# A top-2 expert layer on one core: uneven halves in the second pass, and results sent to their tokens instead of fetched

## The chip, the cores and the metric

The kernel runs on one core of a Trainium2 chip. The metric is the device time of one execution, in microseconds (us). The kernel before has a median of 599.58 us over three runs (596.98 to 600.19).

## The reference, cut to what matters

Input x has 16 x 256 = 4096 tokens of 128 channels. The reference is a sandwich: half an expert layer, attention, and the same half expert layer again.

```python
x = x + 0.5 * ffn(layernorm(x))
x = x + attention(layernorm(x))          # 16 heads of 8, causal over 256 tokens
x = x + 0.5 * ffn(layernorm(x))

def ffn(xt):                             # 16 experts, the best 2 of each token
    logits = xt @ Wg.T + bg
    top_vals, top_idx = top_k(logits, 2)
    rw = softmax(top_vals)
    gate, up = interleaved halves of xt @ Wgu[e] + bgu[e]
    gate, up = minimum(gate, 7.0), clip(up, -7.0, 7.0)
    gated = (up + 1.0) * gate * sigmoid(1.702 * gate)
    return sum over the 2 experts of rw * (gated @ Wd[e] + bd[e])
```

## The kernel before, in words

**Tiles and groups.** The 4096 tokens are 32 tiles of 128. Four tiles are a group, so there are eight groups, 0 to 7 (`NQ`). Each expert layer works on two sides. In both layers a side is four groups: sides 0 and 1 in the first layer, 2 and 3 in the second.

**Routing.** For each group TensorE makes the logits, VectorE finds the two best experts, and from running counts computes for every (token, choice) a row in a DRAM buffer `rows_by_expert`. GpSimd then issues one indirect DMA per tile and choice (`scatter`, L600), eight for a group, which writes 128 normalised token rows to these places. Each expert has a region of its own per side. When a side's counts are known, VectorE makes a table that gives for each tile of expert work its first row and its expert; SyncE copies it into `tab` (L459).

**Expert passes.** A side is 48 expert tiles (32 tiles of choices and one more per expert for padding; 47 are run), two by two in 24 pairs, and four pairs make a turn. For each pair SyncE loads the rows (L467), TensorE transposes them (`turn_x`, L1793), ScalarE copies the transposes out of PSUM (`evac_x`, L883) and brings the weights (L876), TensorE multiplies (`gate_up`, L1805; `down`, L1817), VectorE gates (L1332 to L1335) and adds the bias (`evac_y`, L1349), and ScalarE stores the results to DRAM in tile order (`store`, L895). The five steps run staggered over consecutive slots of one pair each. Every engine's queue is a fixed order, written out by the program; semaphores join them.

**Getting results back.** GpSimd gathers by token: one indirect DMA per tile and choice (`gather`, L535) reads 128 result rows at `tilepos`, a position that VectorE computes for each side (`in_tiles`). In the second layer all 64 gathers come at the end. The 32 of groups 0 to 3 are paced by the pairs of side 3; the 32 of groups 4 to 7 wait until all stores of side 3 have landed. VectorE then adds the two weighted results to x group by group (L1393), and SyncE writes each group out (L511).

**Around the second layer.** Groups 0 to 5 are routed inside the attention's 64 units of work, at units that a table names (`ROUTED`); the table of side 2 is counted at unit 50 and finished at unit 56. Scatters of groups 0 to 5 (0 to 47) are spread over the last two batch pairs of attention. Groups 6 and 7 are routed in the first slots of side 2, and their 16 scatters are paced one to a pair. Side 2's first load waits for the table and the first 32 scatters; side 3's waits for the other 32. The rows' last channel (`LAST`) is not needed as data, since a normalised row sums to zero and the weights are adjusted for it; it holds the constant 1.0 that brings in the biases.

Of the kernel before, what the change touches and what calls it, by code (L numbers as in the profile page):

```python
# [37 lines left out]
REGION = N // SIDES + P  # L38
TILES = TSIDE * TOPK + E
TABW = 2 * TILES  # L40
# [4 lines left out]
PAIRS = TILES // 2  # L45
ALPHA, LIMIT, EPS = 1.702, 7.0, 1e-5
# [26 lines left out]
TABLE_COUNTS, TABLE_SUMS = 50, 56  # L73
# [6 lines left out]
K_Z, K_MQ, K_MK = 338, 466, 594  # L80
K_SEL = K_MK + 2 * P
K_EW = K_SEL + 2 * P
K_W = K_EW + E


def shape_constants():
# [18 lines left out]

    for g in range(2):
# [31 lines left out]
def build_block(nc, x, w_g, g_last, w_gu, up_last, w_d, b_d, attn_last, b_proj, w_attn, w_proj, konst, out):  # L138
    ctx = ExitStack()
    with ctx:  # L140
# [17 lines left out]

        xs = sb("x_resident", [P, QT + NT, C])
# [32 lines left out]
        macc = sb("macc", [P, NQ + SIDES, E], BF16)  # L192
# [80 lines left out]
        def before(q):  # L273
            return q + q // QSIDE
# [72 lines left out]
        s_comb = sem("s_comb")  # L347
        s_out = sem("s_out")
# [84 lines left out]
        def _(sp):  # L433
# [16 lines left out]
            sp.wait_ge(s_pool, 1)  # L450
# [3 lines left out]
            def table_of(p):  # L454
# [3 lines left out]
                for k in range(2):  # L458
                    sp.dma_start(tab[0:1, g, k * TILES:(k + 1) * TILES], tabc[0:TILES, k:k + 1]).then_inc(s_tab, 16)  # L459
                sp.wait_ge(s_tab, 32 * (p + 1))  # L460

            def load(p, t, k, rows):

                beyond_first(sp, s_xTp, p * PAIRS + (t * DUOS + (k + 1 - DUOS)))
                for i in range(tiles_in(t, k)):
                    u = 2 * k + i
                    sp.dma_start(xt[:, u, :], rows_dram[bass.ds(rows[k % 2 * 2 + i], P), :]).then_inc(s_xt[u], 16)  # L467

            def load_turn(p, t):
                for k in range(DUOS):  # L470
                    if k % 2 == 0:
                        rows = registers(nc, sp, tab[0:1, p % SIDES, bass.ds(t * UNROLL + (TILES + 2 * k), 4)], SIDES * E * REGION)
                    load(p, t, k, rows)

            def experts(p):
                if p == SIDES:
                    for t in range(1, TURNS):
# [3 lines left out]
                with sp.Fori(2, TURNS - 1) as t:  # L481
                    load_turn(p, t)
                load_turn(p, TURNS - 1)

            for f in range(2):
# [6 lines left out]
                sp.wait_ge(s_scat[0], 16 * TOPK * TSIDE * (f + 1))  # L492
# [10 lines left out]
                sp.wait_ge(s_scat[1], 16 * TOPK * TSIDE * (f + 1))  # L503
                load_turn(second, 0)
                experts(second)
                if f == 0:
                    stack_pair(sp, 0, 0)

# [6 lines left out]
        def _(pool):  # L515
            nc.gpsimd.memset(zeros[:, :], 0.0).then_inc(s_pool, 1)
# [5 lines left out]
            pool.wait_ge(s_pool, 2)  # L522

            def stored(p):
                for k in range(DUOS):
                    pool.wait_ge(s_store[k], 16 * TURNS * (p + 1))
                pool.wait_ge(s_tilepos, p + 1)
# [64 lines left out]
            def scatter(f, those, paces=None):  # L592

                for j in those:
                    q, c = j // (QUAD * TOPK), j
                    if j % (QUAD * TOPK) == 0:
                        pool.wait_ge(s_pos, f * NQ + q + 1)
# [1391 lines left out]
```

## Time and profile before

| | |
|---|---|
| median of 3 runs | 599.58 us |
| the profiled execution | 599.92 us |
| its span, first to last instruction | 598.1 us |
| PE, DVE, ACT, POOL busy | 454.4, 471.1, 340.0, 342.9 us |
| mean granted TensorE clock | 0.928 |

PE is TensorE, DVE VectorE, ACT ScalarE, POOL GpSimd, SPq SyncE's DMA queue. A timeline row gives start, duration, engine, line, operation, output<-input and count; in brackets stands how long the engine was idle before and what released it. For an indirect DMA the duration on POOL is its making there, not its landing. The chain of waits is the work that ended last, followed back from the end.

### The profile page before, as it was taken

The numbers are of one execution on the slowest core, as the hardware profiler recorded it, in microseconds if no ns is written. First come the engines' busy times: TensorE is split into PE (matmuls) and PEld (weight loads), VectorE is DVE, ScalarE is ACT, GpSimd is POOL, SyncE is SP. The second block draws the span as 40 slices with busy tenths as digits, with TensorE's granted clock in tenths as the row PEclk, the third lists the DMA queues.
The fourth block names the chain that finished last, engine by engine and source line by source line (L and its number), as shares of the span: only waits on it lengthen the run. The fifth ranks groups of instructions, "written<-read, shape, count | busy, mean of one in ns | idle before, by whom it ended". The sixth has DMA issues, their size and how long they took to land.

```text
span 598.1 us, 18906 instructions
## 1 busy us (share of the span) xinstructions
PE 454.4 (76%) x6375; PEld 327.8 (55%) x6375; DVE 471.1 (79%) x2435; ACT 340.0 (57%) x674; POOL 342.9 (57%) x355
## 2 busy tenths in 40 slices
PE   2544699799758898999999898988887889992000
PEld 1443478687544565655666566555566668881000
DVE  6858788688688889798989889888867898888221
ACT  2332478588424667666666768564485778880000
POOL 3777666436346756564646566555573420777773
PEclk9999999899786999999999999999898999997555
DMA  9971366466384749181736455461223445765422
GB/s 258 374 225 49 106 185 187 121 156 159 81 260 119 226 126 268 29 270 43 242 79 195 125 170 155 160 179 44 67 90 98 133 134 154 188 174 136 105 68 65
DMA packets 123446, 89.73 MB, mean 150 GB/s; under 512 B 11745, under 2 KB 115682, under 8 KB 122978
## 3 DMA queue, kind: packets, MB, share of 16 engines
q1 hardware_dynamic: 89282, 59.52, 33.2%
q0 software_dynamic: 8192, 16.79, 10.3%
q10 hardware_dynamic: 25888, 12.34, 7.2%
q8 instruction: 47, 0.77, 0.6%
q14 instruction: 37, 0.30, 0.2%
HBM read 46.93 MB, written 41.68 MB: 148 GB/s over the span
## 4 chain that ended last, share of the span: by engine, by line
PE 38%; DVE 35%; POOL 12%; issue 8%; ACT 3%; DMA 3%; SPq 0%; DVEq 0%; POOLq 0%; ACTq 0%
DVE by_token L943 13%; PE banks L1805 13%; POOL by_token L535 6%; POOL rows_by_expert L600 5%; PE banks L1817 5%; PE banks L1793 4%; PE banks L1411 3%; PE banks L1561 3%; DVE st L1061 1%; DVE gT L1335 1%; DVE upc L1333 1%; DVE sig L1332 1%; DVE maxima L960 1%; DVE ysb L1349 1%; PE banks L1487 1%
## 5 line engine op out<-in xcount | busy, mean ns | idle before, releaser
L600 POOL DMA_INDIRECT rows_by_expert<-by_token,posi x120 | 118.7, 990 | 73.5 <-issue 23.9
L943 DVE CUSTOM_DVE_ANT_0 by_token<-banks,konst_sb 128x256 f32<-128x256 f32 (+1 forms) x512 | 150.6, 353 | 12.7 <-PE banks L1446 10.4
L720 ACT ACTIVATE pT<-banks 128x1536 f32<-128x1536 f32 x64 | 92.9, 1452 | 41.2 <-PE banks L1502 40.6
L1805 PE MATMUL banks<-xT,pT 128*64 128x128 f32 x1504 | 107.3, 286 | 7.3 <-DVE gT L1335 6.1
L535 POOL DMA_INDIRECT yg<-results_by_tile,tilepos x64 | 62.2, 971 | 65.8 <-PE banks L1817 30.0
L876 ACT ACTIVATE pT<-w_experts 128x384 f32 x188 | 88.3, 516 | 18.3 <-PE banks L1817 7.2
L1805 PEld LDWEIGHTS banks<-xT,pT 128*64 128x64 f32 x1504 | 83.8, 141 | 24.2 <-issue 18.6
L535 POOL DMA_INDIRECT by_token<-results_by_tile,tilepos x64 | 61.5, 961 | 40.0 <-DMA results_by_tile<-ysb 20.8
L1817 PE MATMUL banks<-pT,gT 128*64 128x128 f32 x752 | 59.9, 280 | 3.0 <-DVE ysb L1349 3.0
L1349 DVE TENSOR_TENSOR ysb<-banks,w_experts 128x128 f32<-128x128 f32 x188 | 45.7, 284 | 13.0 <-issue 8.4
L1561 PE MATMUL banks<-pT,by_token 128*32 128x256 f32 (+1 forms) x1024 | 55.5, 335 | 0.0
L1332 DVE SCALAR_TENSOR_TENSOR sig<-banks,sig 128x256 f32<-128x256 f32 x96 | 39.8, 414 | 18.9 <-ACT sig L888 17.6
L714 ACT ACTIVATE mT<-banks 128x256 bf16<-128x256 f32 x64 | 24.5, 383 | 47.4 <-PE banks L1462 46.1
L1487 PE MATMUL banks<-q_stack,k_stack 64*128 64x256 bf16 x256 | 49.1, 272 | 0.0
L1817 PEld LDWEIGHTS banks<-pT,gT 128*64 128x64 f32 x752 | 46.1, 141 | 4.0 <-DVE gT L1335 3.0
L1478 PE MATMUL banks<-mT,select 64*128 64x256 bf16 x256 | 47.3, 275 | 0.5 <-ACT pT L720 0.5
L888 ACT ACTIVATE sig<-banks 128x256 f32<-128x256 f32 x96 | 36.2, 377 | 19.8 <-PE banks L1805 16.0
L1793 PE MATMUL banks<-konst_sb,xt 128*128 128x128 f32 x188 | 42.7, 308 | 5.8 <-DMA xt<-rows_by_expert 4.1
L1335 DVE SCALAR_TENSOR_TENSOR gT<-upc,sig 128x256 f32<-128x256 f32 x96 | 43.1, 449 | 3.3
L883 ACT ACTIVATE xT<-banks 128x256 f32<-128x256 f32 x96 | 35.4, 369 | 15.6 <-PE banks L1793 9.3
L943 DVE DVE_READ_ACCUMULATOR2_ANT maxima<- 128x1 f32 x512 | 42.5, 83 | 0.0
L1393 DVE SCALAR_TENSOR_TENSOR x_resident<-by_token,wts,x_resident 128x128 f32<-128x128 f32 x64 | 18.1, 348 | 30.7 <-DMA by_token<-results_by_tile,tilepos 30.4
(167 smaller groups left out, 1011.4 us busy)
## 6 DMA issues: line engine op xcount, KB each, us to landing
xt<-rows_by_expert SPq DMA_DIRECT2D x188, 64.0 KB
results_by_tile<-ysb ACTq DMA_DIRECT2D x92, 128.0 KB
q_stack<-q_by_part SPq DMA_DIRECT2D x32, 256.0 KB, 4.2
k_stack<-k_by_part SPq DMA_DIRECT2D x32, 256.0 KB, 4.5
q_by_part<-q_parts SPq DMA_DIRECT2D x16, 384.0 KB
k_by_part<-k_parts SPq DMA_DIRECT2D x16, 384.0 KB
x_resident<-in_x SPq DMA_DIRECT2D x8, 256.0 KB, 5.9
w_experts<-in_w_gu SPq DMA_DIRECT2D x1, 2048.0 KB, 10.3
```

Source lines behind the costliest of these rows:

```text
L535: pool.indirect_dma_start(out=to[:, j, :], out_offset=None, in_=results_dram[q // QSIDE], in_offset=bass.IndirectOffsetOnAxis(ap=tilepos[: ...
L600: pool.indirect_dma_start(out=rows_dram, out_offset=bass.IndirectOffsetOnAxis(ap=posi[:, c:c + 1], axis=0), in_=rows_of(f, q)[:, j // TOPK ...
L720: nc.scalar.activation(pT[:, s % 2, :], banks[:, 3:6, :].rearrange("p a q -> p (a q)"), ACT.Exp, scale=SCALE).then_inc(a_exp, 1)
L876: last = nc.scalar.activation(w_tile[:, 2 * k + i, :], w_all[:, bass.ds(held[key][k % 2 * 2 + i], EW)], ACT.Identity)
L943: nc.vector.tensor_tensor_reduce(masked[:, (3 * g + qt) * P:(3 * g + 2 * qt + 1) * P], of, lag, 1.0, NEG * NEG_BELOW, ALU.add, ALU.max, by ...
L1335: nc.vector.scalar_tensor_tensor(out=gT[:, k, 0:rows], in0=ups, scalar=1.0, in1=gated, op0=ALU.add, op1=ALU.mult).then_inc(s_gated, 1)
L1349: last = nc.vector.tensor_tensor(ysb[:, k, i, :], bank[6 + k % 2][:, i * C:(i + 1) * C], w_all[:, bass.ds(held[key][k % 2 * 2 + i] + EW, C ...
L1487: nc.tensor.matmul(bank[3 + g % 2][:, c:c + T], k[r, pair, m, o:o + P], q[r, pair, m, o:o + T], start=False, stop=False)
L1561: last = nc.tensor.matmul(bank[6][g * QUARTER:(g + 1) * QUARTER, c + kt * P:c + T], of_head, w, start=j == 0 and kt == 0, stop=j == GRP - ...
L1793: last = nc.tensor.transpose(bank[k % 2][:, i * P:(i + 1) * P], xt[:, 2 * k + i, :], ident)
L1805: last = nc.tensor.matmul(bank[2 + k % 2][h * HALF:(h + 1) * HALF, at:at + P], w_tile[:, 2 * k + i, which * F + h * HALF:which * F + (h + ...
L1817: last = nc.tensor.matmul(bank[6 + k % 2][h * HALF:(h + 1) * HALF, i * C:(i + 1) * C], gT[:, k, i * P + h * HALF:i * P + (h + 1) * HALF], ...
```

## The change

It touches the second layer. Side 2 now has groups 0 to 4 (56 expert tiles, 55 run, 28 pairs in 7 turns) and side 3 groups 5 to 7 (40 tiles, 39 run, 20 pairs in 5 turns). Before a group of side 2 is scattered, GpSimd writes into the rows' last channel, as an integer, the place of this (choice, token) in a new DRAM buffer `results_by_token`. The expert tiles of side 2 keep their rows in SBUF (`xt`, `yg` and `by_token`, all idle then), and ScalarE turns the last channel into 1.0 as it copies the transposes. VectorE writes the results into the idle `q_stack` and `k_stack` instead of a four-pair buffer, ScalarE stores nothing, and GpSimd sends each tile by an indirect DMA, whose offsets are the last channel of the rows themselves (`send`). Padding rows hold a place beyond the buffer, which a bounds check leaves out. SyncE then loads the results of groups 0 to 4 with ten plain DMAs. Groups 5 to 7 are gathered as before.

```diff
+SIDE_QUADS = ((0, QSIDE), (QSIDE, NQ), (0, 5), (5, NQ))
...
-TABLE_COUNTS, TABLE_SUMS = 50, 56
+TABLE_COUNTS, TABLE_SUMS = 56, 59
...
-            nc.gpsimd.memset(zeros[:, :], 0.0).then_inc(s_pool, 1)
+            nc.gpsimd.memset(zeros[:, 0:LAST], 0.0).then_inc(s_pool, 1)
...
-            pool.wait_ge(s_pool, 2)
+            pool.wait_ge(s_const, 48)
+            nc.gpsimd.tensor_copy(zeros[:, LAST:C].bitcast(I32), kci[:, K_DUMP:K_DUMP + 1]).then_inc(s_pool, 1)
+            pool.wait_ge(s_pool, 3)
...
             def scatter(f, those, paces=None):
...
+                    if f == 1 and side_of(f, q) == 0:
+                        i, choice = j % QUAD, j // QUAD % TOPK
+                        c = (q * QUAD + i) * TOPK + choice
+                        if i == 0:
+                            if j == 0:
+                                pool.wait_ge(s_scat[1], 16 * TOPK * TSIDE)
+                            pool.wait_ge(s_scat[0], 16 * (TOPK * TSIDE + j))
+                            at = (SLOTS * QT * GRP * VW + 3 * GRP * P) // C + q * QUAD
+                            ids = K_TOKEN + choice * SENT_TILES + q * QUAD
+                            nc.gpsimd.tensor_copy(by_token_i[:, at:at + QUAD, LAST], kci[:, ids:ids + QUAD]).then_inc(s_token, 1)
+                            pool.wait_ge(s_token, q * TOPK + choice + 1)
...
+            def send(tile):
+
+                t, u = tile // UNROLL, tile % UNROLL
+                pool.wait_ge(s_ysb[u // 2], FIRST_TURN[SIDES] + t + 1)
+                pool.indirect_dma_start(
+                    out=by_token_dram, out_offset=bass.IndirectOffsetOnAxis(ap=token_of(t, u), axis=0),
+                    in_=result_of(tile), in_offset=None,
+                    bounds_check=TOPK * SENT_TILES * P - 1, oob_is_err=False).then_inc(s_sent if t else s_sent_first, 16)
...
-                    scatter(1, of_quads(6, 8), [(s_y, 2 * PAIRS + 1 + j) for j in range(2 * QUAD * TOPK)])
-
-                    for q in range(NQ):
-                        if q % QSIDE == 0:
-                            stored(SIDES + q // QSIDE)
-                        paces = [(s_y, 3 * PAIRS + 4 + (q * QUAD * TOPK + j) * 2 // 3) for j in range(QUAD * TOPK)] if q < QSIDE else None
-                        gather(q, last_results[:, q * QUAD * TOPK:(q + 1) * QUAD * TOPK, :], s_got[q], range(QUAD * TOPK), paces)
+                    left = of_quads(MERGED, NQ)
+                    for x in range(SENT // 2 + 1):
+                        scatter(1, left[x:x + 1])
+                        for tile in range(2 * x, min(2 * x + 2, SENT)):
+                            send(tile)
+
+                    stored(SIDES + 1)
+                    for q in range(SIDE_QUADS[2][1], NQ):
+                        gather(q, last_results[:, q * QUAD * TOPK:(q + 1) * QUAD * TOPK, :], s_got[q], range(QUAD * TOPK))
...
             # SyncE, behind all its loads
+            sp.wait_ge(s_sent_first, 16 * UNROLL)
+            sp.wait_ge(s_sent, 16 * (SENT - UNROLL))
+            of_choice = by_token_dram.rearrange("(k n p) c -> k p n c", k=TOPK, p=P)
+            for q in range(SIDE_QUADS[2][1]):
+                for k in range(TOPK):
+                    sp.dma_start(last_results[:, q * QUAD * TOPK + k:(q + 1) * QUAD * TOPK:TOPK, :],
+                                 of_choice[k, :, q * QUAD:(q + 1) * QUAD, :]).then_inc(s_got[q], 16)
...
             # SyncE, ahead of side 2's first load, and of side 3's
-                sp.wait_ge(s_scat[0], 16 * TOPK * TSIDE * (f + 1))
+                sp.wait_ge(s_scat[0], 16 * TOPK * QUAD * (QSIDE + f * SIDE_QUADS[2][1]))
...
-                sp.wait_ge(s_scat[1], 16 * TOPK * TSIDE * (f + 1))
+                sp.wait_ge(s_scat[1], 16 * TOPK * QUAD * (QSIDE + f * (NQ - SIDE_QUADS[2][1])))
...
             # ScalarE, evac_x
+                    if p == SIDES:
+                        nc.scalar.activation(xT[:, k % 2, 0:rows], bank[k % 2][:, 0:rows], ACT.Identity, bias=kc[:, K_ONE:K_ONE + 1],
+                                             scale=kc[:, K_KEEP:K_KEEP + 1]).then_inc(s_xT, 1)
...
             # ScalarE, store
+                    if p == SIDES:
+                        return
```

GpSimd's order from the last scatters of attention to the end, before (`rows_by_expert<-` is a scatter, `by_token<-results_by_tile` a gather; `rstd` the root for group 7):

```order
L600 DMA rows_by_expert<-by_token,posi 69760x128 [waits a_pv,s_pos]
L600 DMA rows_by_expert<-by_token,posi 69760x128 [waits a_pv] x7
L587 TENSOR_TENSOR rstd<-veps,neghalf 128x4 [waits s_veps]
L600 DMA rows_by_expert<-by_token,posi 69760x128 [waits s_y,s_pos]
L600 DMA rows_by_expert<-by_token,posi 69760x128 [waits s_y] x7
L600 DMA rows_by_expert<-q_rest,posi 69760x128 [waits s_y,s_pos]
L600 DMA rows_by_expert<-q_rest,posi 69760x128 [waits s_y] x7
L535 DMA by_token<-results_by_tile,tilepos 128x128 [waits s_store3,s_tilepos,s_store2,s_y,s_store1,s_store0]
L535 DMA by_token<-results_by_tile,tilepos 128x128 [waits s_y] x31
L535 DMA by_token<-results_by_tile,tilepos 128x128 [waits s_store3,s_store2,s_tilepos,s_store1,s_store0]
L535 DMA by_token<-results_by_tile,tilepos 128x128 x31
```

And now, its beginning and its end (`results_by_token<-` is a send):

```order
L666 DMA rows_by_expert<-by_token,posi 86144x128 [waits a_pv,s_pos]
L666 DMA rows_by_expert<-by_token,posi 86144x128 [waits a_pv] x7
L642 TENSOR_TENSOR rstd<-veps,neghalf 128x4 [waits s_veps]
L666 DMA rows_by_expert<-by_token,posi 86144x128 [waits s_pos]
L674 DMA results_by_token<-q_stack,xt 5120x128 [waits s_ysb0] x2
L666 DMA rows_by_expert<-by_token,posi 86144x128
L674 DMA results_by_token<-q_stack,xt 5120x128 [waits s_ysb1] x2
...
L674 DMA results_by_token<-k_stack,by_token 5120x128 [waits s_ysb2] x2
L674 DMA results_by_token<-k_stack,by_token 5120x128 [waits s_ysb3]
L590 DMA by_token<-results_by_tile,tilepos 128x128 [waits s_store3,s_store2,s_tilepos,s_store1,s_store0]
L590 DMA by_token<-results_by_tile,tilepos 128x128 x23
```

Between two scatters of groups 6 and 7 there now stand two sends. With 16 scatters, 55 sends and 24 gathers GpSimd makes 95 indirect DMAs here, where it made 80.

GpSimd's order for group 4, before (scatters 32 to 39, with the root for group 6 among them):

```order
L600 DMA rows_by_expert<-by_token,posi 69760x128 [waits a_max,s_pos]
L600 DMA rows_by_expert<-by_token,posi 69760x128 [waits a_max] x4
L587 TENSOR_TENSOR rstd<-veps,neghalf 128x4 [waits s_veps]
L600 DMA rows_by_expert<-by_token,posi 69760x128 [waits a_max] x2
L600 DMA rows_by_expert<-by_token,posi 69760x128 [waits a_pv]
```

And now:

```order
L662 COPY by_token<-konst_sb 128x4 [waits s_scat0,s_pos]
L666 DMA rows_by_expert<-by_token,posi 86144x128 [waits a_max,s_token]
L666 DMA rows_by_expert<-by_token,posi 86144x128 [waits a_max] x3
L662 COPY by_token<-konst_sb 128x4 [waits s_scat0]
L666 DMA rows_by_expert<-by_token,posi 86144x128 [waits a_max,s_token]
L642 TENSOR_TENSOR rstd<-veps,neghalf 128x4 [waits s_veps]
L666 DMA rows_by_expert<-by_token,posi 86144x128 [waits a_max] x2
L666 DMA rows_by_expert<-by_token,posi 86144x128 [waits a_pv]
```

Ahead of every four scatters of side 2 stands a copy that waits until all of the side's scatters so far have landed; there are ten.

## Rows read from the trace of the kernel before

**Rows 1.** Windows: busy us of each engine, granted clock, DMA share.

```profile
core 0: us, PE busy (x) PEld busy (x) DVE busy (x) ACT busy (x) POOL busy (x), PEclk, DMA share, GB/s
...
520.00:540.00 20.00, 20.00 (x297) 16.67 (x293) 17.78 (x57) 16.56 (x44) 15.12 (x17) 1.00 0.67 171
...
560.00:580.00 20.00, 0.00 (x0) 0.00 (x0) 4.56 (x16) 0.00 (x0) 15.23 (x16) 0.50 0.31 79
```

**Rows 2.** Chain of waits, 538 to 599 us: start, us, what.

```profile
core 0 of [0], span 598.1 us
by line: POOL by_token L535 54.4%; issue 19.9%; DMA by_token<-results_by_tile,tilepos 4.1%; DVE x_resident L1393 3.3%; POOLq L140 2.0%; PE banks L1805 1.7%; DVE sig L1332 1.0%; DVE upc L1333 0.9%; DVEq L1892 0.8%; DVE gT L1335 0.8%; PE bank
...
589.00 2.52 DMA by_token<-results_by_tile,tilepos
```

**Rows 3.** Same chain at the start of side 1, first layer.

```profile
108.06 2.63 DMA rows_by_expert<-by_token,posi
...
111.72 2.49 DMA xt<-rows_by_expert
...
114.35 0.41 PE banks L1793 x2
```

**Rows 4.** Same chain at the start of side 0, first layer.

```profile
60.06 2.22 DMA rows_by_expert<-by_token,posi
...
66.87 0.66 PE banks L1793 x2
```

**Rows 5.** GpSimd's timeline, 425 to 488 us; brackets: idle before, releaser.

```profile
425.52 0.97 POOL L600 DMA_INDIRECT rows_by_expert<-by_token,posi  x1 [0.30 <-issue]
428.25 0.96 POOL L600 DMA_INDIRECT rows_by_expert<-by_token,posi  x1 [1.76 <-DVE maxima L960]
...
432.15 1.02 POOL L600 DMA_INDIRECT rows_by_expert<-by_token,posi  x1 [1.59 <-DVE maxima L960]
...
434.76 0.97 POOL L600 DMA_INDIRECT rows_by_expert<-by_token,posi  x1 [0.30 <-issue]
436.04 0.96 POOL L600 DMA_INDIRECT rows_by_expert<-by_token,posi  x1 [0.30 <-issue]
...
444.95 0.97 POOL L600 DMA_INDIRECT rows_by_expert<-by_token,posi  x1 [0.30 <-issue]
...
451.92 1.03 POOL L600 DMA_INDIRECT rows_by_expert<-by_token,posi  x1 [4.15 <-DVE posi L1151]
...
487.47 0.96 POOL L600 DMA_INDIRECT rows_by_expert<-q_rest,posi  x1 [2.17 <-PE banks L1817]
```

**Rows 6.** GpSimd's timeline, first gather for group 4.

```profile
550.00 1.01 POOL L535 DMA_INDIRECT by_token<-results_by_tile,tilepos  x1 [0.30 <-issue]
```

**Rows 7.** TensorE's timeline: transposes of rows, sides 2 and 3.

```profile
439.56 0.38 PE L1793 MATMUL banks<-konst_sb,xt 128*128 128x128 f32 x2
...
494.44 0.33 PE L1793 MATMUL banks<-konst_sb,xt 128*128 128x128 f32 x1
...
496.16 0.44 PE L1793 MATMUL banks<-konst_sb,xt 128*128 128x128 f32 x2
...
499.38 0.44 PE L1793 MATMUL banks<-konst_sb,xt 128*128 128x128 f32 x2
...
537.59 0.33 PE L1793 MATMUL banks<-konst_sb,xt 128*128 128x128 f32 x1
```

**Rows 8.** TensorE's timeline: third transposes of side 1, first layer.

```profile
119.11 0.44 PE L1793 MATMUL banks<-konst_sb,xt 128*128 128x128 f32 x2
```

**Rows 9.** ScalarE's timeline: the last two stores of results.

```profile
543.55 0.90 ACTq L895 DMA_DIRECT2D results_by_tile<-ysb  x2
```

**Rows 10.** VectorE's timeline: constants landed; combining of groups 0 to 3.

```profile
5.54 0.24 DVE L1047 CAST tri<-konst_sb 128x128 bf16<-128x128 f32 x1 [0.18 <-DMA konst_sb<-in_konst]
...
545.10 9.04 DVE L1393 SCALAR_TENSOR_TENSOR x_resident<-by_token,wts,x_resident 128x128 f32<-128x128 f32 x32
```

**Rows 11.** Groups of instructions, 439 to 540 us: last step of the gate.

```profile
L1335 DVE SCALAR_TENSOR_TENSOR gT<-upc,sig 128x256 f32<-128x256 f32 (+1 forms) x46 | 19.6, 427 | 1.6
```

More of the change, by code:

```diff
@@ L45 @@
 PAIRS = TILES // 2
+TURNS_OF = tuple(((hi - lo) * QUAD * TOPK + E) // UNROLL for lo, hi in SIDE_QUADS)
+FIRST_TURN = tuple(sum(TURNS_OF[:p]) for p in range(2 * SIDES + 1))
+FIRST_PAIR = tuple(turn * DUOS for turn in FIRST_TURN)
+STORED_TURNS = (0, TURNS, 2 * TURNS, 2 * TURNS, 2 * TURNS + TURNS_OF[3])
+SENT = TURNS_OF[SIDES] * UNROLL - 1
 ALPHA, LIMIT, EPS = 1.702, 7.0, 1e-5
@@ L104, in shape_constants @@
         k[:, K_MK + half * P:K_MK + (half + 1) * P] = np.where(p[None, :] > half * HALF + p[:, None] % HALF, NEG, 0)
+    k[:, K_DUMP] = (TOPK * SENT_TILES * P + p).astype(np.int32).view(np.float32)
+    k[:, K_KEEP], k[:, K_ONE] = p < LAST, p == LAST
+    for n in range(TOPK * SENT_TILES):
+        k[:, K_TOKEN + n] = (n * P + p).astype(np.int32).view(np.float32)
     for g in range(2):
@@ L271, in rows_of, with side_of, before, result_of @@
             return by_token[:, at:at + QUAD * C].rearrange("p (n c) -> p n c", c=C)
-        def before(q):
-            return q + q // QSIDE
+        def side_of(f, q):
+            return int(q >= SIDE_QUADS[2 * f][1])
+        def before(f, q):
+            return f * (NQ + SIDES) + q + side_of(f, q)
+        kci = kc.bitcast(I32)
+        by_token_i = by_token.bitcast(I32).rearrange("p (n c) -> p n c", c=C)
+        sent = [of.rearrange("p a m t -> p (a m t)").bitcast(F32).rearrange("p (n c) -> p n c", c=C) for of in stack]
+        def result_of(tile):
+            return sent[tile // NT][:, tile % NT, :]
+        def x_tile(p, t, u):
+            if p != SIDES or t == 0:
+                return xt[:, u, :]
+            if t == 1:
+                return a_yg[:, u, :]
+            return by_token[:, ((t - 2) * UNROLL + u) * C:((t - 2) * UNROLL + u + 1) * C]
+        def token_of(t, u):
+            return x_tile(SIDES, t, u)[:, LAST:C].bitcast(I32)
         def xnT_of(f, q):
@@ L471, in load_turn @@
                     if k % 2 == 0:
-                        rows = registers(nc, sp, tab[0:1, p % SIDES, bass.ds(t * UNROLL + (TILES + 2 * k), 4)], SIDES * E * REGION)
+                        rows = registers(nc, sp, tab[0:1, p % SIDES, bass.ds(t * UNROLL + (MOST + 2 * k), 4)], SIDES * E * REGION)
                     load(p, t, k, rows)
@@ L476, in experts @@
                 if p == SIDES:
-                    for t in range(1, TURNS):
+                    for t in range(1, TURNS_OF[p]):
                         load_turn(p, t)
@@ L1128, in spread_mask @@
                     ch.wait()
[L1129 removed]
+                    nc.vector.tensor_tensor(macc[:, before(f, q) + 1, :], macc[:, before(f, q), :], msum[:, q, :], ALU.add).then_inc(s_mask, 1)
                 def top2(q):
@@ L1933, in expert_passes @@
         peeled = 2 if p == 1 else 1
+        turns = TURNS_OF[p]
         if p == SIDES:
-            for t in range(TURNS):
+            for t in range(turns):
                 turn(p, t)
@@ L1939, in expert_passes @@
         turn(p, 1)
-        with eng.Fori(2, TURNS - peeled) as t:
+        with eng.Fori(2, turns - peeled) as t:
             if chain:
@@ L1944, in expert_passes @@
         if chain:
-            chain[0].end(TURNS - peeled - 2)
-        for t in range(TURNS - peeled, TURNS):
+            chain[0].end(turns - peeled - 2)
+        for t in range(turns - peeled, turns):
             turn(p, t)
     for k in range(max(behind for behind, _ in steps)):
-        slot(f * SIDES + 1, TURNS, k)
+        slot(f * SIDES + 1, TURNS_OF[f * SIDES + 1], k)
 _OUT = (B, T, C)
```

143 lines of the change are left out of this document (81 added, 62 removed).

## The prediction

> **What bounds the kernel now.** I read the windows first, then the chain of waits of the last 60 us, then GpSimd's timeline. The windows show three regimes: while side 3 passes TensorE is full (20.00 of 20 us), and afterwards TensorE and ScalarE do nothing while GpSimd makes DMAs [rows 1]. In the last 60 us more than half of the chain is GpSimd's gathers (54.4%), plus "issue", the 0.30 us between two of them [rows 2]. Their pitch is the price that everything below goes by: the 32 gathers of groups 4 to 7 start at 550.00 [rows 6], the last at 589.00 [rows 2], so (589.00 - 550.00) / 31 = 1.26 us each, 40.3 us in all. Scatters in a row go at the same pace: from 436.04 to 444.95 there are seven steps [rows 5], 1.27 us each. So an indirect DMA costs GpSimd 1.27 us, of either kind. In side 2 GpSimd has room: its 16 scatters lie between 451.92 and 487.47 [rows 5], 2.4 us apart, as the pairs allow.
>
> **What the change takes away.** The tail has 24 gathers where it had 32: 8 x 1.26 = 10.1 us less. In addition, 550.00 is late by itself: the last store of side 3 is issued in the second half of 543.55 to 544.45 [rows 9], and GpSimd was still busy with group 3's gathers then. The gathers of groups 0 to 3 are gone, so the 24 can start as soon as the last store has landed. ScalarE's 28 stores of side 2 and one of VectorE's two position computations go too; I give nothing for them, as neither engine will be the bound in side 2 (below). The ten plain loads wait for the last send and are hidden under the 24 gathers, as is VectorE's combining of five groups: four took 9.04 us [rows 10], five take 11.3, against 30 us of gathers.
>
> **What it adds, step by step.**
>
> *Start.* GpSimd now waits for the constants before its first root. They are there when VectorE's first use starts, at 5.54 us [rows 10]; a copy of one column and its semaphore follow. The root started at 5.51, so I take +0.3 us (0 to 0.6).
>
> *Choice waits.* Each set of four scatters of side 2 waits until the set before it has landed. Landing takes 2.2 to 2.6 us from the scatter's start [rows 3, 4]. Where it counts is group 4: scatter 35 starts at 425.52, scatter 36 at 428.25 [rows 5], so this wait just fits; if scatter 35 is itself 1.3 us late from an earlier wait, 36 starts at 429.7. Then a root and scatter 37 follow, which attention releases at 432.15 anyway [rows 5]. I take +0.2 us for the last scatter of group 4; up to 1.5 if each landing takes 2.9 us. The other eight waits lie where GpSimd waits for attention.
>
> *Side 2 starts later.* Its first load now needs 40 scatters, not 32. The 40th starts at 434.76 [rows 5], with the above 434.96. From a side's last scatter to its first transposes the first layer shows 6.3 us [rows 3] and 6.8 us [rows 4]: landing, the table's registers, load, landing. So the first transposes come at 441.3 instead of 439.56 [rows 7]: +1.7 us (0.9 to 3). Behind them in TensorE's queue stand group 6's logits and the last batch's projection, for which VectorE's positions of group 6 wait, so GpSimd's first scatter of group 6 moves with them: 451.92 + 0.3 + 1.7 = 453.9.
>
> *GpSimd becomes the bound of side 2.* From there the order is scatter, send, send, and so on. The results are there in time, since a pair needs 1.8 us (the 21 pair steps from 499.38 to 537.59 [rows 7]) and GpSimd three DMAs, 3.8 us. Side 3's load waits for the 16th scatter, with 15 scatters and 30 sends ahead of it: 453.9 + 45 x 1.27 = 511.1, where it was 487.47 [rows 5]. First transposes of side 3: 511.1 + 6.3 = 517.4, where they were at 496.16 [rows 7]: +21.2 us. Four of these pairs are useful work moved from side 3 to side 2 (4 x 1.82 = 7.3 us), and 2.0 us is the later start; the rest, about 12 us, is TensorE waiting. The trace has no send. For it the scatter stands as the nearest row; it writes 128 rows of 512 B by an index from SBUF too, but checks no bound and reads another tensor. Bounds: below, a send could cost only the 0.95 us of work without the gap; above, I add 0.2 us.
>
> *Side 3.* It has 20 pairs instead of 24: -7.3 us. It starts after a stall. In the first layer, side 1 after its stall needs 4.76 us from its first to its third transposes (114.35 to 119.11) [rows 3, 8], side 3 now 3.22 (496.16 to 499.38) [rows 7]: +1.5 us. The last store thus shifts by 21.2 - 7.3 + 1.5 = 15.4, from 544.0 to 559.4. It lands some 2.5 us later (no row shows it; 2.2 to 2.6 for the scatters [rows 3, 4]), and the first gather starts at 562.0: +12.0 against 550.00. GpSimd's last send, the 25th behind the 16th scatter, starts at 511.1 + 25 x 1.27 = 543, long before.
>
> *Sum.* +12.0 - 10.1 = +1.9 us on the start of the last gather (590.9). From there to the end it is 598.1 - 589.0 = 9.1 us [rows 2], as before. The profiled execution took 599.92, so 601.8; the median lies 0.3 lower: **601.5 us**. All rests on 45 DMAs in a row: the sum is zero at 1.23 us each instead of 1.27.
>
> **Rivals.**
>
> *A. Sends are dearer.* The bound is compared for 128 indices, and a row's last channel is read at a step of 512 B. GpSimd's small operations cost a fraction of a microsecond, so 0.1 to 0.2 us per send: 30 of them ahead of the 16th scatter, +3 to +6, 604.5 to 607.5 us. This is the one on the slower side: at its place the stall grows to 15 or 18 us, and it decides from 0.04 us per send on (+1.1, past the 0.5%). Against it: scatters and gathers differ by 0.01 us though they do different things.
>
> *B. Sends are cheaper, or GpSimd is not the bound.* If GpSimd made a send in 0.95 us, 30 x 0.32 = 9.6 us go: 592 us. At the end of this lies the case without any stall: side 3's transposes at 505.5, and the stall and its cold start of 13.4 us gone: 588 us. For it: padding rows need no write, and the seven unused tiles none at all. Against it: the pitch is GpSimd's own, not the transfer's, for the transfers are spread over the engines' 67% busy share [rows 1] and the pitch is the same at 31%.
>
> *C. The waits for landing hold attention.* GpSimd also makes roots that VectorE needs. If the landings take 3 us or more beside attention's traffic, group 4's last scatter is 2 to 3 us late, and so is all behind it: 604 us.
>
> *D. VectorE holds GpSimd off.* The 45 DMAs lie beside gates whose last step reads two tensors from SBUF and takes 0.43 us [rows 11]. If each DMA lost one such step, 45 x 0.43 = 19 us would be added: 621 us. Against it: with VectorE busy 17.78 of 20 us GpSimd starts 17 DMAs, with VectorE at 4.56 us it starts 16 [rows 1]. The Trainium skill, page "SBUF — State Buffer", section "Who interferes with whom", says that a DMA made by GpSimd can't get its descriptors written while VectorE holds the port pair that the two share, in a two-port operation. By that rule this change, which puts 55 more such DMAs beside the gates, is the wrong direction; by these rows the gates hardly do that.
>
> *E. It does not do what it says:* the sends' landing, not their making, is waited for somewhere, or the loads come after the gathers. SyncE waits for the sends only behind all its loads of side 3, so this would cost nothing that the 30 us of gathers do not cover: about 601.
>
> **Chances.** A difference under 0.5% (3 us) can't be told from none here; so faster is below 596.6, slower above 602.6. Forecast 0.54, its own range 598.5 to 604.5; of it 0.39 falls within 0.5% and 0.15 above, since 601.5 is near that edge. A 0.18, slower. B 0.16, of it 0.15 faster. C 0.07, slower. D 0.02, slower. E 0.03, same. Sum: faster 0.15, same 0.43, slower 0.42. Range: 595 to 609 takes in the forecast's own, A, C and the near part of B.
>
> **What would show it.** Side 2's first transposes near 441.6; GpSimd without a gap from about 454 to 544, in threes 3.8 us apart; TensorE idle some 12 us before side 3, first transposes near 517, at a lower granted clock at first; the first gather near 562 and 24 of them; sends' mean beside the scatters' 0.96. The prediction is wrong if the 16th scatter starts before 505 (B) or after 514 (A), or if side 2 starts over 3 us late (C).

## The result and the profile after

The changed kernel takes 607.32 us (median of 4 runs, 606.59 to 610.24), the kernel before beside it 599.26: ratio 1.0162, 95% interval 1.0117 to 1.0208. It is slower by 1.6%. Forecast were 601.5 us, a range of 595 to 609, and 0.43 for "no difference" against 0.42 for "slower". The profiled execution took 606.59 us with a span of 604.8; the forecast for such an execution was 601.8 with a span of 600.0. So 4.8 us are to be explained.

GpSimd's timeline of the changed kernel, second layer. L666 is the scatter, L674 the send, L590 the gather.

```profile
453.79 1.02 POOL L666 DMA_INDIRECT rows_by_expert<-by_token,posi  x1 [4.07 <-DVE posi L1234]
455.91 1.10 POOL L674 DMA_INDIRECT results_by_token<-q_stack,xt  x1 [1.10 <-issue]
457.31 0.99 POOL L674 DMA_INDIRECT results_by_token<-q_stack,xt  x1 [0.30 <-issue]
...
511.83 0.98 POOL L674 DMA_INDIRECT results_by_token<-q_stack,by_token  x1 [0.30 <-issue]
513.12 0.97 POOL L666 DMA_INDIRECT rows_by_expert<-q_rest,posi  x1 [0.30 <-issue]
...
545.56 0.97 POOL L674 DMA_INDIRECT results_by_token<-k_stack,by_token  x1 [0.30 <-issue]
565.90 0.99 POOL L590 DMA_INDIRECT by_token<-results_by_tile,tilepos  x1 [19.37 <-DMA results_by_tile<-ysb]
```

Between the first scatter of group 6 and the last send there is no gap but the 0.30 us of issue and one of 1.10 ahead of the first send. The 16th scatter starts at 513.12, where it was 487.47 [rows 5]. The sends take about as long as the scatters, as the groups of instructions, 453 to 604 us, show (busy time, mean ns of one):

```profile
L674 POOL DMA_INDIRECT results_by_token<-k_stack,by_token x23 | 22.9, 994 | 7.0 <-issue 7.0
...
L666 POOL DMA_INDIRECT rows_by_expert<-by_token,posi x8 | 8.2, 1019 | 6.2 <-DVE posi L1234 4.1 <-issue 1.8 <-DVE q_stack L1436 0.3
L666 POOL DMA_INDIRECT rows_by_expert<-q_rest,posi x8 | 7.8, 981 | 2.4 <-issue 2.4
```

TensorE's transposes of rows answer to [rows 7]: the start of side 2, the end of it, the first three and the last of side 3.

```profile
441.15 0.41 PE L1880 MATMUL banks<-konst_sb,xt 128*128 128x128 f32 x2 [0.93 <-DMA xt<-rows_by_expert]
...
500.90 0.33 PE L1880 MATMUL banks<-konst_sb,by_token 128*128 128x128 f32 x1
518.74 0.66 PE L1880 MATMUL banks<-konst_sb,xt 128*128 128x128 f32 x2 [16.06 <-DMA xt<-rows_by_expert]
521.24 0.69 PE L1880 MATMUL banks<-konst_sb,xt 128*128 128x128 f32 x2
524.62 0.66 PE L1880 MATMUL banks<-konst_sb,xt 128*128 128x128 f32 x2
...
555.73 0.33 PE L1880 MATMUL banks<-konst_sb,xt 128*128 128x128 f32 x1
```

Side 3 waits 16.06 us for its first load, and is slow for its first pairs. The windows, with the columns of [rows 1], show the same; the clock stands at 0.50, the lower of its two levels (1.2 GHz), when the pairs start again:

```profile
505.00:518.00 13.00, 0.00 (x0) 0.00 (x0) 0.00 (x0) 0.00 (x0) 9.91 (x11) 0.62 0.17 57
518.00:525.00 7.00, 6.26 (x46) 4.88 (x46) 1.88 (x7) 2.43 (x7) 5.22 (x6) 0.50 0.49 144
...
550.00:560.00 10.00, 8.39 (x125) 6.84 (x121) 8.46 (x28) 6.39 (x17) 0.00 (x0) 1.00 1.04 299
```

The chain of waits shows what released whom at the two places where the sum was made: between the 16th scatter and side 3, and at the end. The answer to 589.00 in [rows 2] is 595.09.

```profile
513.12 2.24 DMA rows_by_expert<-q_rest,posi
...
516.66 1.95 DMA xt<-rows_by_expert
518.74 0.66 PE banks L1880 x2
...
557.47 5.51 DMA results_by_tile<-ysb
...
563.43 1.56 DMA results_by_tile<-ysb
...
565.90 0.99 POOL by_token L590
...
595.09 2.54 DMA by_token<-results_by_tile,tilepos
```

At the end there is something that wasn't forecast. A store of results issued at 557.47 takes 5.51 us to land. SyncE's and VectorE's timelines show what lies beside it: the ten plain loads of by_token, 256 KB each, are issued from 549.44 on, and VectorE waits for the store to free its buffer.

```profile
549.44 8.97 SPq L559 DMA_DIRECT2D by_token<-results_by_token  x10
```

```profile
561.85 0.49 DVE L1436 TENSOR_TENSOR ysb<-banks,w_experts 128x128 f32<-128x128 f32 x2 [0.85 <-DMA results_by_tile<-ysb]
563.11 0.29 DVE L1436 TENSOR_TENSOR ysb<-banks,w_experts 128x128 f32<-128x128 f32 x1 [0.77 <-DMA results_by_tile<-ysb]
```

### The profile page after: what moved, and what is told of

The parts are those of the page before. It is cut to its first block, busy times and chain, and to the rows that moved or that the text cites. A ratio compares the mean times of both kernels' runs of the same rounds, so it can differ in the third digit from the quotient of the medians.

```text
span 604.8 us, 18891 instructions
## 1 busy us (share of the span) xinstructions
PE 456.2 (75%) x6375; PEld 328.8 (54%) x6375; DVE 470.4 (78%) x2432; ACT 343.4 (57%) x674; POOL 362.3 (60%) x381
## 4 chain that ended last, share of the span: by engine, by line
PE 33%; DVE 29%; POOL 16%; issue 11%; DMA 5%; ACT 3%; SPq 1%; POOLq 0%; DVEq 0%; ACTq 0%
DVE by_token L1026 13%; PE banks L1892 10%; POOL rows_by_expert L666 7%; PE banks L1904 4%; POOL results_by_token L674 4%; PE banks L1880 4%; POOL by_token L590 4%; PE banks L1646 3%; PE banks L1496 3%; DMA xt<-rows_by_expert 1%; DMA rows_by_expert<-by_token,posi 1%; DVE st L1144 1%; PE banks L1669 1%; DMA results_by_tile<-ysb 1%; PE banks L1572 1%
## 5 line engine op out<-in xcount | busy, mean ns | idle before, releaser
L666 POOL DMA_INDIRECT rows_by_expert<-by_token,posi x120 | 120.2, 1002 | 54.3 <-issue 25.8
L590 POOL DMA_INDIRECT yg<-results_by_tile,tilepos x64 | 62.0, 969 | 63.0 <-DVE maxima L1043 26.1
L1880 PE MATMUL banks<-konst_sb,xt 128*128 128x128 f32 x141 | 32.5, 313 | 23.4 <-DMA xt<-rows_by_expert 21.3
L1531 PE MATMUL banks<-k_stack,q_stack 64*128 64x128 bf16 x256 | 37.2, 227 | 6.2 <-ACT mT L791 3.4
L1436 DVE TENSOR_TENSOR ysb<-banks,w_experts 128x128 f32<-128x128 f32 x133 | 32.3, 284 | 11.8 <-issue 6.6
L1418 DVE TENSOR_SCALAR upc<-banks 128x256 f32<-128x256 f32 x96 | 39.1, 407 | 0.0
L590 POOL DMA_INDIRECT by_token<-results_by_tile,tilepos x24 | 23.1, 964 | 26.4 <-DMA results_by_tile<-ysb 19.4
```

The source lines that it names most:

```text
L590: pool.indirect_dma_start(out=to[:, j, :], out_offset=None, in_=results_dram[q // QSIDE], in_offset=bass.IndirectOffsetOnAxis(ap=tilepos[: ...
L666: pool.indirect_dma_start(out=rows_dram, out_offset=bass.IndirectOffsetOnAxis(ap=posi[:, c:c + 1], axis=0), in_=rows_of(f, q)[:, i, :], in ...
L1880: last = nc.tensor.transpose(bank[k % 2][:, i * P:(i + 1) * P], x_tile(p, t, 2 * k + i), ident)
```

## The experiments

My theory: GpSimd's DMAs in a row decide when the 16th scatter starts, and by it when side 3 starts. The rivals were that a DMA with a bound checked is dearer by itself, and that the loss lies in the landing of loads and stores at the end. Twelve more runs were made, of seven kernels (one of them the change itself), on four chips. On two of these the kernel before takes 598 us, close to the 599 above; on the two others it takes 683 to 684. Ratios are to the kernel before on the same chip, and only those of one chip are compared with each other.

**The scatters ahead of the sends.** 30 sends stood ahead of the 16th scatter; here there are 8.

```
-                    for x in range(SENT // 2 + 1):
-                        scatter(1, left[x:x + 1])
-                        for tile in range(2 * x, min(2 * x + 2, SENT)):
-                            send(tile)
+                    scatter(1, left[0:8])
+                    for tile in range(8):
+                        send(tile)
+                    scatter(1, left[8:16])
+                    for tile in range(8, SENT):
+                        send(tile)
```

> The changed kernel with GpSimd's order in side 2 altered alone: 8 scatters of group 6, 8 sends, 8 scatters of group 7, then the other 47 sends. Theory 1 (the 30 sends ahead of the 16th scatter hold side 3 back): the 16th scatter starts at about 483 us instead of 513.1, TensorE's 16 us wait before side 3 goes, side 3's first transposes come at about 503 instead of 518.7, the last store lands near 548, the first of the 24 gathers starts at 547 to 550 (GpSimd is then free from its sends too, 55 + 16 DMAs at 1.29 us from 454), and the time is 587 to 592 us, below the kernel before. Rival (the sends as such, by their DMA traffic or by VectorE and GpSimd hindering each other, slow the passes, or the later start of side 2 is the cause): the same 55 sends are made, so side 3 ends about as late and the time stays above 600.

It ran on a chip on which the kernel before takes 683.45 us, and took 719.22: ratio 1.0527 (1.0473 to 1.0582). Three others ran there with it, and TensorE was held up in ways that the first chip doesn't show (last section); GpSimd isn't the limit there, for it waits 36.09 us ahead of its first gather. So it was run again, with the change itself beside it.

> The changed kernel as it is, beside the kernel before on the same chip, since the four kernels before this ran on a chip on which the kernel before needs 683 us and not 599, and TensorE waits for its instructions there. If the chip is like the first one: 605 to 608 us, a ratio of 1.010 to 1.018. If it is like the second: near 718, ratio 1.05, as for the same kernel with another order of scatters and sends.

> The kernel of e1_scatters_first once more, beside the changed kernel itself. Theory 1 on a chip like the first: side 3's first transposes at about 503 us, no wait of 16 us, the first gather at 547 to 550, 587 to 592 us. On a chip like the second, where the passes themselves are slow: equal to the changed kernel within 1%, as GpSimd is not the last to be ready there.

The kernel before took 597.79 us there. The change took 607.93, ratio 1.0184 (1.0151 to 1.0217): the result holds. With the scatters first it took **586.95 us, ratio 0.9817 (0.9785 to 0.9849)**, so this order beats both kernels, by 21 us and by 11. It was expected at 587 to 592. Its GpSimd timeline and its transposes follow; every edit moves the line numbers a little, and here the transposes stand in L1882:

```profile
465.56 1.00 POOL L674 DMA_INDIRECT results_by_token<-q_stack,xt  x1 [0.30 <-issue]
...
485.11 0.97 POOL L666 DMA_INDIRECT rows_by_expert<-q_rest,posi  x1 [0.30 <-issue]
486.39 0.99 POOL L674 DMA_INDIRECT results_by_token<-q_stack,yg  x1 [0.30 <-issue]
...
545.65 0.98 POOL L674 DMA_INDIRECT results_by_token<-k_stack,by_token  x1 [0.30 <-issue]
547.49 1.00 POOL L590 DMA_INDIRECT by_token<-results_by_tile,tilepos  x1 [0.86 <-DMA results_by_tile<-ysb]
...
576.67 0.94 POOL L590 DMA_INDIRECT by_token<-results_by_tile,tilepos  x1 [0.30 <-issue]
```

```profile
442.65 0.41 PE L1882 MATMUL banks<-konst_sb,xt 128*128 128x128 f32 x2 [0.82 <-DMA xt<-rows_by_expert]
...
502.60 0.33 PE L1882 MATMUL banks<-konst_sb,by_token 128*128 128x128 f32 x1
504.32 0.44 PE L1882 MATMUL banks<-konst_sb,xt 128*128 128x128 f32 x2
...
507.54 0.44 PE L1882 MATMUL banks<-konst_sb,xt 128*128 128x128 f32 x2
...
538.43 0.33 PE L1882 MATMUL banks<-konst_sb,xt 128*128 128x128 f32 x1
```

The same number of DMAs, the same sends, and yet the 16th scatter starts 28.0 us earlier, the wait ahead of side 3 is gone (502.60, then 504.32), and the two profiled spans differ by 604.8 - 586.3 = 18.5 us. All of it can be accounted for. Side 3 starts 14.4 us earlier (518.74 to 504.32) though side 2 started 1.5 later; it needs 5.88 us to its third transposes in the change and 3.22 here, and with its other pairs this makes 2.9 (36.99 against 34.11 for the side); from the last transposes to the first gather 10.17 against 9.06, 1.1; the rest is equal within 0.1. The first theory stands.

GpSimd's rows say the same from the other end. The last of the 71 scatters and sends starts at 545.56 in the change and at 545.65 here. What differs is how long GpSimd then waits for side 3's last store: 19.37 us there, 0.86 here, and these 18.5 us are the whole difference. They also show how little is left: from its first scatter of group 6 (455.27) to its last gather (576.67) GpSimd is idle here for nothing but the 0.30 us between two DMAs and these 0.86. With the same 95 DMAs a better order, or a faster TensorE in these passes, could gain about 1 us more.

**Part of the sends taken from ahead.** 23 instead of 30 (after each scatter two sends and one by turns).

```
-                        for tile in range(2 * x, min(2 * x + 2, SENT)):
-                            send(tile)
+                        for _ in range(2 - x % 2):
+                            if tile < SENT:
+                                send(tile)
+                                tile += 1
```

> The changed kernel with two sends and one send in turn between the scatters, so that 23 sends instead of 30 stand ahead of the 16th scatter. Theory 1: the 16th scatter starts 7 x 1.29 = 9.0 us earlier, at 504.1, side 3's first transposes at 509.7, and the time falls by 9 us from the changed kernel's, to about 598 us (TensorE still waits, about 7 us). Rival (traffic or hindrance): hardly a difference.

> Left out: nothing. 23 of the 39 sends stand ahead of the 16th scatter, where the change has 30 and scatters_first 8. If GpSimd's count of DMAs ahead of the 16th scatter sets the start of the last side (first theory), it falls on a line between the two: 7 sends less at 1.285 us each is 9.0 us earlier than 513.1, so 504.1, the side's first transposes near 509.7 after a wait of some 7 us, and the time some 8 to 9 us under the change's, near 598 to 599 beside a kernel before of 598. If the time lost lies in the ten plain loads and the store's landing (second theory), it stays at 605 to 608. If the last side starts early only when no send stands among the scatters (third, contention by interleaving), it also stays above 604.

Both runs fell on chips of the other kind: 721.41 us, ratio 1.0572 (1.0517 to 1.0627), and 729.75 beside 684.46, ratio 1.0667 (1.0611 to 1.0723). TensorE was held up there by something else, and GpSimd isn't the limit: in the second run it waits for VectorE's results in the middle of its sends (5.04 us at 570.84) and 41.01 us ahead of its first gather. So neither run tells the theories apart. A measured middle point is lacking, and with it a separate test of whether sends that stand between the scatters do harm beyond their number; the unchanged pitch of the DMAs speaks against it.

**The ten plain loads after the last store.** SyncE waits for side 3's stores ahead of them.

```
+            for k in range(DUOS):
+                sp.wait_ge(s_store[k], 16 * STORED_TURNS[2 * SIDES])
```

> The changed kernel, but SyncE issues the ten loads of 256 KB only when all stores of side 3 have landed. Theory 2 (the loads stand in the way of the last stores: a store took 5.5 us to land, VectorE waited twice for it, and the first gather started 10.2 us after the last transposes where 9.0 were forecast): stores land in about 2.5 us, the first gather starts some 1.2 to 2 us earlier, and the time falls by 1 to 2 us, to 604.5 to 606. The loads then go beside the gathers and stay hidden. Rival: the loads only use idle time; no difference, or the gathers become slower by their traffic and the gain is lost.

> The kernel of e4_loads_after_stores once more, beside the changed kernel itself: 1 to 2 us below it if the ten loads hold back the last stores (theory 2), with a last store that lands in about 2.5 us; equal to it otherwise.

On the slower chip: 718.22 us, 1.0518 (1.0464 to 1.0571). On a chip like the first: 605.27 us, 1.0124 (1.0085 to 1.0163), beside 607.93 for the change. The intervals overlap; the trace says more (TensorE, GpSimd and VectorE in turn):

```profile
555.96 0.33 PE L1882 MATMUL banks<-konst_sb,xt 128*128 128x128 f32 x1
```

```profile
564.95 1.00 POOL L592 DMA_INDIRECT by_token<-results_by_tile,tilepos  x1 [17.52 <-DMA results_by_tile<-ysb]
```

```profile
568.79 13.61 DVE L1480 SCALAR_TENSOR_TENSOR x_resident<-by_token,wts,x_resident 128x128 f32<-128x128 f32 x48 [5.34 <-DMA by_token<-results_by_token]
```

From the last transposes to the first gather it is 8.99 us, against 10.17 in the change (and 10.33 in its second run, 554.03 to 564.36). So the loads cost 1.2 to 1.3 us by lying beside the last stores. The kernel with the scatters first agrees: there they go out at 547.83, behind the last store, and the way takes 9.06 us. In this run VectorE waits for the loads afterwards (the 5.34 us above), and that is hidden beneath the gathers. This is a small part of the loss.

**A bound checked on every indirect DMA.** Scatters and gathers get a bounds_check that no index passes.

```
+                        bounds_check=P + SIDES * E * REGION - 1, oob_is_err=False).then_inc(...)
```

> The changed kernel, with the bounds check of the sends given to every scatter and gather too (a bound that no index passes). If the check is what makes a send dearer than a scatter (0.98 against 0.965 us), scatters come to 0.98 us and gathers to 0.965; if it is the sends' offsets or tensors, they stay. The time moves by less than 2 us either way, which one look can't tell.

One run, 614.25 us, where less than 2 us of difference from the change was expected. Its groups of instructions over the whole span:

```profile
L667 POOL DMA_INDIRECT rows_by_expert<-by_token,posi x120 | 119.8, 998 | 60.5 <-issue 26.9 <-PE banks L1882 10.6 <-DVE maxima L1045 8.6
L590 POOL DMA_INDIRECT yg<-results_by_tile,tilepos x64 | 65.2, 1018 | 70.3 <-DVE maxima L1045 29.1 <-issue 21.7 <-PE banks L1906 18.7
L590 POOL DMA_INDIRECT by_token<-results_by_tile,tilepos x24 | 24.8, 1033 | 25.8 <-DMA results_by_tile<-ysb 18.7 <-issue 7.0
```

In the change the same groups have 1002, 969 and 964 ns. A scatter isn't dearer with a bound, and a send is a scatter of the same size; a gather is dearer, by 0.05 to 0.07 us, but the gathers of the change carry no bound. From the first scatter of group 6 to the end this run takes 151.4 us (460.89 to 612.3) and the change 151.0 (453.79 to 604.8), so in the stretch in which the time is lost the bounds change nothing. The run loses its 7 us before that; why is not shown, and its whole time is not used.

**The sides without the sends.** Sides of five and three groups, but every result is stored and gathered, 40 and then 24, after all 16 scatters.

```
-                    for x in range(SENT // 2 + 1):
-                        scatter(1, left[x:x + 1])
...
+                    scatter(1, left, [(s_y, 2 * PAIRS + 1 + j) for j in range(2 * QUAD * TOPK)])
+                    for q in range(NQ):
+                        if q in (0, SIDE_QUADS[2][1]):
+                            stored(SIDES + side_of(1, q))
```

> One part alone: sides of five and three groups, but side 2's results stored in tile order and gathered by token, 40 gathers paced by side 3's pairs and then 24, no index in the rows and no send. If the sizes of the sides cost by themselves: side 2's first transposes at about 441, side 3's at about 504 without a wait, the first gather some 7 to 8 us later than before (509.2), so near 517, then 64 x 1.26 us without a gap, the last starting at 597, 606 to 608 us in all: GpSimd's gathers alone set the end, and the longer first side only starts them later. Against it: if the sends are what costs, this version is no slower than the kernel before (599).

> Left out: nothing. The sides of five and three groups, but every result gathered by GpSimd after its store, as before: 40 gathers stand ahead of the 16th scatter's place only if they are asked for there; here all 16 scatters come first, then 40 gathers of the first side, then 24. First theory: no wait ahead of the last side; 4 fewer tile pairs for the last side are behind the last store; TensorE ends some 11 to 12 us earlier than the change (last store lands near 545 to 547), 24 gathers from there, 0.98 of before or a few us above, 587 to 592, provided that the 40 gathers are done by then (16th scatter near 475, 40 at 1.27 us is 526). Rival: sends and not sides brought what scatters_first gains; then this one is at before's time, 597 to 600.

> Left out: nothing. The same kernel as gathers_only_again (sides of five and three groups, all results gathered by GpSimd, 40 and then 24, no send), for a chip whose kernel before is near 598. First theory: the 16 scatters are done near 475 and nothing holds the last side; its first transposes follow side 2 near 504, the last store lands near 547, 24 gathers from there, 587 to 592. Rival: it takes the sends to bring the gain, since with 40 gathers asked for after the first side's stores GpSimd is not done in time; then 595 to 600. On a chip whose kernel before is near 684, where the versions with sends took 718 to 730, both theories expect what was measured there before, 683 to 689.

On the two slower chips: 682.70 us, ratio 1.0014 (0.9980 to 1.0049), and 688.85, 1.0056 (1.0026 to 1.0085). On a chip like the first: 608.12 beside 597.89, **ratio 1.0181 (1.0109 to 1.0254)**. My number for the last one (587 to 592) was wrong; its rival named the right side, but its 595 to 600 were too low as well. The expectation written first for this kernel had it: the first gather near 517, the last at 597, 606 to 608 us in all. Its rows (GpSimd, then TensorE's last transposes), and below them one of the kernel before:

```profile
489.72 0.96 POOL L652 DMA_INDIRECT rows_by_expert<-q_rest,posi  x1 [1.93 <-PE banks L1888]
518.78 0.98 POOL L576 DMA_INDIRECT by_token<-results_by_tile,tilepos  x1 [28.10 <-DMA results_by_tile<-ysb]
...
598.71 0.95 POOL L576 DMA_INDIRECT by_token<-results_by_tile,tilepos  x1 [0.30 <-issue]
```

```profile
539.85 0.33 PE L1864 MATMUL banks<-konst_sb,xt 128*128 128x128 f32 x1
```

```profile
509.23 1.00 POOL L535 DMA_INDIRECT by_token<-results_by_tile,tilepos  x1 [20.80 <-DMA results_by_tile<-ysb]
```

TensorE is done early, and it is worth nothing: 64 gathers in a row need 80 us from the moment at which side 2's last store has landed, whatever side 3 does. In the kernel before that moment is 509.23, and 589.00 [rows 2] is 63 steps of 1.27 later; here it is 518.78, since the larger side is stored later, and 598.71 is 63 steps of 1.27 later as well. The difference, 9.6 to 9.7 us, is nearly all of the loss (608.12 - 597.89 = 10.2 between the medians). So GpSimd bounds the kernel before too, from 509 us to the end; I had used this for the start at 550.00 but hadn't followed it back to 509. What the sends give is that GpSimd works on results while side 2 still makes them. Before, it stood idle for 20.80 us ahead of its first gather, besides the waits between its paced scatters; so 95 DMAs can end earlier than 80.

**Even sides with sends.** Four and four groups, 47 sends where the change has 55, 32 gathers, scatters first. The expectation below counts 31 and 39 sends, and one above 39; the traces have 47 and 55.

```
-SIDE_QUADS = ((0, QSIDE), (QSIDE, NQ), (0, 5), (5, NQ))
-SENT_TILES = 5 * QUAD
+SIDE_QUADS = ((0, QSIDE), (QSIDE, NQ), (0, QSIDE), (QSIDE, NQ))
+SENT_TILES = 4 * QUAD
```

> Left out: nothing. Sends by carried index as in the change, in the order of scatters_first, but sides of four and four groups: 31 sends instead of 39, and 32 gathers at the end instead of 24. First theory: no wait ahead of the last side, its first transposes as before near 496 to 498, the last store lands near 547 to 549, then 32 gathers at 1.26 us (40.3) and 9.5 of the end: 597 to 599, the kernel before's time within 0.5%. What scatters_first gains over it (10 to 11 us) is then the eight gathers moved off the end (10.1). Rival: the gain comes from the sends themselves; then this is also near 587 to 590.

It ran only on a slower chip, where 597 to 599 us don't apply: 727.40 us, ratio 1.0645 (1.0599 to 1.0692), and doesn't tell what the sides alone are worth.

## Why the prediction came out as it did

The mechanism was right and each place of it was found: GpSimd without a gap from 454 us, side 3 held by the 16th scatter, a colder TensorE behind it, and the ten microseconds of gathers more than given back by the stall. The number was 4.8 us short by five terms, each read from the rows above.

- *45 DMAs at 1.27 us.* First scatter 453.79 (forecast 453.9), the 16th at 513.12 (511.1): +2.0. The 45 steps took 59.33 us instead of 57.15. The first send waits 0.80 us longer than the 0.30 between two others, with no releaser named. Its result had been written some 4 us before, from 450.93 on, and the same 1.10 stands in five more runs of this order; what it waits for is open. The other 1.4 us are 0.03 us on each step, half of it in seven longer DMAs of 1.02 to 1.21 us, scatters and sends alike. Sends have a mean of 0.99 us where I had 0.96 from the scatter. Put on the 30 sends alone it would be 0.05 us each, just past rival A's threshold of 0.04, but the scatters among them are longer than 0.96 too (means 1.02 and 0.98 for the two groups). The 0.1 to 0.2 us that rival A priced did not come, and that a checked bound is the reason of the rest isn't shown (with bounds on all, scatters were not dearer).
- *From scatter to transposes, 6.3 us.* 5.62 (518.74 - 513.12): -0.7. Landing, registers and load again, each a little shorter than in [rows 3].
- *Cold start, 1.5 us.* From the first to the third transposes 5.88 us, where the first layer's second side had 4.76 [rows 3, 8]: +1.1; the rest of the side is 0.3 slower. The wait was 16 us, not 12, because I had put side 2's end too late: four more pairs lengthened it by 5.1 us (442.65 to 504.32 is 61.7 in the kernel with the scatters first, 56.6 from 439.56 to 496.16 before [rows 7]), not by 7.3. The forecast didn't depend on that, rival B did: for no stall at all I gave 588 us, and the kernel without it took 586.95.
- *The last store, 9.0 us from the last transposes to the first gather.* 10.17: +1.2. "The ten plain loads are hidden under the 24 gathers" failed. They start when the last load of side 3 and the sends allow, at 549.44, ahead of the gathers and on top of the last stores. Loads after the stores gave 8.99.
- *Gathers and end.* 23 steps took 29.19 us (28.9), +0.3, and from the last gather to the end 9.71 us instead of 9.1, +0.6. The kernel with the scatters first has 9.63 there, so the stall isn't its cause; the one without sends has 8.5. From the last gather to the end of VectorE's last addition these three and the kernel before take 4.9 us alike. The difference lies behind that: 4.8 us in the two with sends, 4.2 before and 3.7 without sends. What makes it is open.

Together 2.0 - 0.7 + 1.4 + 1.2 + 0.3 + 0.6 = 4.8. Of the other steps, the start (16.73 against 16.34 for the first scatter, +0.4) and group 4's last scatter (435.25, forecast 434.96) were right within 0.3; side 2's first transposes, forecast 441.3, came at 441.15. Rival C fell with them. Rival D fell with the pitch: for 45 DMAs beside the gates it wanted 0.43 us more on each, and 0.03 came. By the Trainium skill's page "SBUF — State Buffer", section "Who interferes with whom", VectorE operations with two inputs in SBUF disturb a GpSimd instruction that reads SBUF. Most of the 0.03 us is not of that kind. Side 3's late start leaves a stretch in which VectorE does nothing, and the pitch is the same there: 9 steps from 505.40 to 516.98 take 1.29 us each, and so do 10 from 487.33 to 500.19 beside a busy VectorE (columns of [rows 1]). Whether the seven longer DMAs are of that kind, no run shows.

```profile
487.33:500.19 12.86, 12.86 (x188) 10.49 (x186) 11.63 (x37) 11.91 (x30) 9.82 (x10) 1.00 0.30 92
505.40:516.98 11.58, 0.00 (x0) 0.00 (x0) 0.00 (x0) 0.00 (x0) 8.84 (x10) 0.61 0.14 50
```

The chances were set too near to "no difference". The sum had no reserve for a stall that is dearer than its length, and three of the five terms (cold start, crowded end, first send) are of the kind that can only add.

## What to carry to other kernels

When work is handed to an engine that makes DMAs in order, count what stands ahead of the one DMA that the next stage waits for, and put that one first: the same 55 sends made this kernel 1.6 to 1.8% slower with 30 of them ahead of that DMA, and 1.8% faster with 8. An engine with a run of equal DMAs that starts at one event bounds the kernel from that event on, if the run outlasts the work beside it, and however idle the engine looked before; moving work off its run gains only if the run can start earlier or gets shorter. Plain loads issued beside the last stores of a stage delay them, even when the loads themselves are not needed yet.

## What the runs showed of the hardware

An indirect DMA of 128 rows of 512 B takes GpSimd 0.95 to 1.0 us and 0.30 us between two, whether it gathers, or scatters to rows or to tokens; with a bound a gather took 0.05 to 0.07 us more in the one run that has it, and a scatter no more.

Large plain loads lengthen the landing of what lies beside them, and not its making. With the scatters first, the gathers made between 547 and 557 us, beside the ten loads of 256 KB, landed in 5.5 us (median, 3.5 to 6.1), the later ones in 2.6; their pitch was 1.29 us and then 1.26.

Not expected at all: two other chips ran the kernel before in 683 to 684 us, the one without sends at 1.0014 and 1.0056 of that, and all five runs with sends at 1.05 to 1.07, in whatever order; the change itself didn't run there. TensorE's groups on one of these chips, 500 to 680 us, with the scatters first (the first two) and without sends (the last two), busy time, mean ns, then idle time before them:

```profile
L1894 PE MATMUL banks<-xT,pT 128*64 128x128 f32 x752 | 66.5, 307 | 29.2 <-issue 19.6 <-ACT xT L963 9.2
L1906 PE MATMUL banks<-pT,gT 128*64 128x128 f32 x376 | 38.6, 304 | 9.8 <-issue 7.3 <-DVE ysb L1438 2.5
```

```profile
L1876 PE MATMUL banks<-xT,pT 128*64 128x128 f32 x752 | 55.5, 293 | 9.1 <-ACT xT L949 3.9 <-DVE gT L1403 3.4 <-issue 1.7
L1888 PE MATMUL banks<-pT,gT 128*64 128x128 f32 x376 | 30.4, 277 | 2.0 <-issue 1.5 <-DVE ysb L1418 0.5
```

With sends the same multiplies wait 27 us for nothing that the profile shows, and without them 3.2. That TensorE lacked instructions there is a guess; no run isolates it, and whether it is the chip or what else ran on it stays open. For a kernel that must run on any chip it means that the scatters first, 1.8% faster on one, are 5% slower on another.
